# Reordering the opening of a conv-plus-FFN kernel, and the chunk work at its step ends

## The reference, cut to what matters

```
y   = grouped_conv1d(x, weight (128,32,9), groups=4, padding 4)   # x: (32 samples, 128 channels, 2048)
y   = y + (c @ c_weight.T)[:, :, None] + bias[None, :, None]
out = x + y @ kernel + ffn_bias                                   # kernel: (2048, 2048)
        + B_eff (A_eff y) + lora_B_shared (lora_A_shared y)
# A_eff, B_eff: one mix per group of 4 samples of 16 low-rank adapters (rank 32), weights `gate` (8,16)
```

## Time and profile before

| | |
|---|---|
| time, median of 3 runs | 1790.21 us (1789.97 to 1790.29) |
| profiled execution, its own time | 1793.14 us |
| its span, first to last instruction | 1791.3 us |
| mean granted clock of PE, share of full | 0.976 |
| PE busy | 1736.4 us, 97% |
| DVE, ACT, POOL busy | 1016.6, 669.3 and 189.5 us |
| moved by transfers | 411.22 MB |

### The profile page before, as it was taken

The page is one execution under the profiler, slowest core; times in us unless marked ns, Lnnn a source line. Parts: engine busy times, 40 slices in busy tenths (PEclk is TensorE's granted clock), DMA queues, the critical chain, the costliest instruction groups (busy, mean ns, idle before and its releaser), DMA issues.

```text
span 1791.3 us, 21987 instructions
## 1 busy us (share of the span) xinstructions
PE 1736.4 (97%) x8710; PEld 1487.9 (83%) x8710; DVE 1016.6 (57%) x1179; ACT 669.3 (37%) x841; POOL 189.5 (11%) x70
## 2 busy tenths in 40 slices
PE   6799899999999997999999999999999999999999
PEld 6688788878888887999999888888888888888887
DVE  3676765653544459999998423345555544453333
ACT  4556565653422256555564211122222311121110
POOL 0023422220000002222332100000000000000000
PEclk6699999999999998999999999999999999999999
DMA  8578768763666554887776654457776799886654
GB/s 213 152 245 286 254 224 276 260 207 118 203 222 218 198 186 172 327 299 277 259 250 247 224 191 148 178 179 243 240 229 217 246 338 315 307 287 206 195 197 149
DMA packets 182287, 411.22 MB, mean 230 GB/s; under 512 B 58724, under 2 KB 94404, under 8 KB 177544
## 3 DMA queue, kind: packets, MB, share of 16 engines
q1 hardware_dynamic: 182184, 409.81, 67.5%
HBM read 263.72 MB, written 146.03 MB: 229 GB/s over the span
## 4 chain that ended last, share of the span: by engine, by line
PE 87%; DVE 5%; DMA 4%; issue 2%; ACT 1%; SPq 1%; DVEq 0%; ACTq 0%
PE acc L1202 64%; PE cps L1104 14%; PE cps L1134 3%; PE acc L1120 3%; DVE x_q L838 2%; PE acc L1173 2%; DMA T<-g 2%; DMA mixed_B<-b_raw 2%; DVE g L862 1%; PE cps L1229 1%; DMA g<-in_L_ffn_lora_B_shared 1%; DVE x_lo L845 1%; ACT x_q L663 0%; ACT w_hi L655 0%; PE cps L1218 0%
## 5 line engine op out<-in xcount | busy, mean ns | idle before, releaser
L1202 PE MATMUL acc<-w_hi,y_t 128*128 128x512 f32 x3584 | 998.8, 393 | 10.0 <-DVE w_lo L828 6.9
L1202 PEld LDWEIGHTS acc<-w_hi,y_t 128*128 128x128 f32 x3584 | 669.4, 189 | 145.8 <-DVE w_lo L828 7.4
L1202 PE MATMUL acc<-w_lo,y_t 128*128 128x512 f32 x1792 | 556.2, 392 | 0.0
L1202 PEld LDWEIGHTS acc<-w_lo,y_t 128*128 128x128 f32 x1792 | 338.9, 189 | 71.8
L663 ACT COPY x_q<-x_raw 32x512 f32<-32x512 f32 x256 | 276.7, 1081 | 52.0 <-DVE x_lo L845 44.6
L1104 PE MATMUL cps<-cw_hi,x_hi 128*128 128x384 f32 (+2 forms) x768 | 232.2, 302 | 5.4 <-DVE x_lo L845 5.4
L1104 PE MATMUL cps<-cw_lo,x_hi 128*128 128x384 f32 (+2 forms) x768 | 232.0, 302 | 0.0
L1104 PE MATMUL cps<-cw_hi,x_lo 128*128 128x384 f32 (+2 forms) x768 | 231.3, 301 | 0.0
L692 ACT CAST y_t<-g 128x1024 fp32r<-128x1024 f32 x96 | 101.1, 1053 | 343.1 <-PE acc L1202 314.2
L927 DVE TENSOR_TENSOR g<-acc,g 128x1024 f32<-128x1024 f32 x96 | 117.0, 1220 | 171.5 <-PE acc L1120 113.0
L888 DVE TENSOR_TENSOR y_t<-g,y_t 128x1024 fp32r<-128x1024 f32 x96 | 119.4, 1244 | 133.2 <-ACT y_t L692 133.2
(11 more groups left out here) (94 smaller groups left out, 1057.2 us busy)
## 6 DMA issues: line engine op xcount, KB each, us to landing
g<-U SPq DMA_DIRECT2D x80, 512.0 KB, 5.7
x_raw<-in_x SPq DMA_DIRECT2D x32, 1024.0 KB, 6.4
g<-A SPq DMA_DIRECT2D x64, 512.0 KB, 5.2
g<-in_x SPq DMA_DIRECT2D x64, 512.0 KB, 6.3
out<-g SPq DMA_DIRECT2D x64, 512.0 KB, 3.4
A<-g SPq DMA_DIRECT2D x48, 512.0 KB, 5.1
S<-g SPq DMA_DIRECT2D x48, 512.0 KB, 3.0
U<-g SPq DMA_DIRECT2D x48, 512.0 KB, 4.1
```

The lines of the kernel that those rows point to most:

```text
L1202: ins = T.matmul(acc[:, b, m, :], y_buf[b][:, c, part, :], wt[:, k % SLOTS, m * 512:(m + 1) * 512], start=(c == 0 and part == 0 and wt is ...
```

## The change

The arithmetic stays the same apart from buffers and order.

- **Opening.** The first sample is loaded by ACT's queue. SP issues the small inputs, lora_A_shared, weight chunks 0 to 3 and then one slice of lora_A. The sample is rearranged and split group by group (`rearrange_0`, `split_0`), DVE taking 10 of the 16 copies and ACT 6, and `conv(0)` waits for one group at a time. PE then runs `conv(0)`, `mix_A(0)`, product 0, `mix_A(1)`, `conv(1)`, `mix_A(2)`, the transposes of the first lora_B slice, `mix_A(3)`, L1229, and the loop starts at step 1. `ax_part(0)` moves into product 1, after its third chunk. `mix_A(1)` writes banks of `cps` instead of `acc`.
- **lora_B_shared** is loaded, transposed, copied and stored in step 15 instead of in the opening.
- **Splits.** The `EARLY_SPLIT` chunks go to the end of a step on both engines. In step 31, the only step p = 15 that is followed by a convolution, chunks 3 and 4 join 5 to 7 at the end. The permuting copy of lora_B moves on ACT from before `x_split` to after `y_hi`.
- **Forming.** One call at each step's end, from step 1 to step 9: first the stores of chunk u-2, then the loads of chunk u-1.
- **Waits.** `ax_part(u)` waits for three of the four evacuated groups.

```diff
@@ SP, at each step's end
-            def forming(point):
-                j, part = (point - 1) // 3, (point - 1) % 3
-                if point >= 1 and j < NCH:
-                    if part == 0:
-                        load_forming(j)
-                    elif part == 2:
-                        store_formed(j)
+            def forming(u):
+                if 2 <= u <= NCH + 1:
+                    store_formed(u - 2)
+                if 1 <= u <= NCH:
+                    load_forming(u - 1)
@@ SP, opening
-            load_x(0)
...
-            load_lora_A(0)
-            load_lora_A(1)
             sp.dma_start(As_raw, lora_As).then_inc(as_raw_in, 16)
-            sp.dma_start(Bs_raw.rearrange("p (k r) -> p k r", r=RANK),
-                         lora_Bs.rearrange("(k p) r -> p k r", p=P)).then_inc(bs_raw_in, 16)
             for c in range(4):
                 load_t(0, c)
+            load_lora_A(0)
             sp.wait_ge(ctx_ready, 1)
             sp.dma_start(ctx_d, ctx_sum).then_inc(ctx_out, 16)
             sp.wait_ge(ctx_out, 16)
             load_ctx(0)
             load_ctx(1)
             load_x(1)
             for c in range(4, NCH):
                 load_t(0, c)
+            sp.wait_ge(as_done, 1)
+            load_lora_A(1)
+            load_lora_B(0)
+            store_y(0)
+            store_mixed_A(0)
+            load_lora_A(2)
+            load_x(2)
...
@@ ACT, opening
+            act.dma_start(x_raw[:], x[0]).then_inc(x_in, 16)
...
+            rearrange_0(0, (3,)).then_inc(q0_act, 1)
+            rearrange_0(1, (2,))
+            split_0(0)
+            rearrange_0(1, (3,)).then_inc(q0_act, 1)
+            split_0(1)
...
@@ DVE, opening
+            rearrange_0(0, (0, 1, 2))
+            rearrange_0(1, (0, 1))
+            split_0(0)
+            rearrange_0(2, (0, 1, 2))
+            split_0(1)
+            rearrange_0(3, (0, 1))
+            split_0(2)
+            split_0(3)
...
+            for i in range(GR):
+                split_t(0, i)
+                y_group(0, i)
+            y_lo(0)
+            for c in range(4, NCH):
+                split_t(0, c)
             a_mixed_copy(0)
             x_rearrange(1)
             x_split(1)
@@ PE, opening
-            mix_A(0)
-            mix_A(1)
-            conv(0)
-            mix_A(2)
-            mix_A(3)
-            pe.wait_ge(amix_act, RK)
-            pe.wait_ge(amix_dve, RK)
+            conv(0)
+            mix_A(0)
+            pe.wait_ge(gcol_ready, 1)
+            product(0)
+            mix_A(1)
+            conv(1)
+            mix_A(2)
+            turn_lora_B(0)
+            mix_A(3)
+            mix_B(0)
@@ DVE, a step
-                if f + 1 < 7 and p == NP - 1:
+                if f + 1 < 7 and p == NP - 1 and not has_conv(u + 1):
                     split_t(f + 1, 3)
                     split_t(f + 1, 4)
                 if has_conv(u + 2):
                     x_rearrange(conv_index(u + 2))
-                if f + 1 < 7 and p in EARLY_SPLIT:
-                    split_t(f + 1, EARLY_SPLIT[p])
...
+                if f + 1 < 7 and p in EARLY_SPLIT:
+                    split_t(f + 1, EARLY_SPLIT[p])
                 if f + 1 < 7 and p == NP - 1:
-                    for c in range(5, NCH):
+                    for c in range(3 if has_conv(u + 1) else 5, NCH):
                         split_t(f + 1, c)
@@ PE, ax_part
-                    pe.wait_ge(y_evac, min(4 * (u + 2), 4 * NP))
+                    pe.wait_ge(y_evac, min(4 * max(u + 1, 2) + 3, 4 * NP))
```

More of the change, by code:

```diff
@@ L568, in _ @@
                     load_sums(u + 1)
-                if u >= 1 and early(pu):
+                if early(pu):
                     store_stage(pu)
@@ L744, in _ @@
-            for c in range(4):
-                split_t(0, c)
-            a_mixed_copy(2)
-            a_mixed_copy(3)
-            y_hi(0)
+                    act.wait_ge(cwt_done, 3)
+                elif k >= 2:
+                    act.wait_ge(amix_out[k % 2], 32 * (k // 2))
+                src = cps[:, 3, :] if k == 1 else acc[:, 1, 0, :]
+                A.copy(a_stage[k % 2][:, 0].rearrange("p b (c r) -> p b c r", c=NCH),
+                       src.rearrange("p (c b r) -> p b c r", c=NCH, b=NB)).then_inc(amix_act, 1)
@@ new lines, in _ @@
+            act.wait_ge(x_in, 16)
+            act.wait_ge(edge_zero, 2)
+            rearrange_0(0, (3,)).then_inc(q0_act, 1)
[3 more added lines that the diff above has]
+            split_0(1)
+            rearrange_0(2, (3,)).then_inc(q0_act, 1)
+            split_0(2)
+            rearrange_0(3, (2, 3)).then_inc(q0_act, 1)
+            split_0(3)
+            for c in range(5):
+                split_t(0, c)
+            y_hi(0)
@@ L749, in _ @@
+            for c in range(5, NCH):
+                split_t(0, c)
+            a_mixed_copy(0)
             x_rearrange(1)
             x_split(1)
-            for c in range(4, NCH):
-                split_t(0, c)
-            for u in range(NU):
+            perm_lora_B(0)
+            a_mixed_copy(1)
+            x_rearrange(2)
+            x_split(2)
+            y_hi(1)
+            a_mixed_copy(2)
+            copy_turn(0)
+            a_mixed_copy(3)
+            for u in range(1, NU):
@@ L994, in _ @@
                 ins.then_inc(ones_ready, 1)
-            for c in range(4, NCH):
-                split_t(0, c)
-            for u in range(NU):
+            a_mixed_copy(1)
+            x_rearrange(2)
+            y_evacuate(1)
+            x_split(2)
+            y_lo(1)
+            a_mixed_copy(2)
+            a_mixed_copy(3)
+            copy_mixed_B(0)
+            for u in range(1, NU):
                 f, p = u // NP, u % NP
                 pu, pf = u - 1, (u - 1) // NP
-                if u >= 1 and pf in (2, 3):
+                if pf in (2, 3):
                     evac(pu)
-                if u >= 1 and pf in (1, 4):
+                if pf in (1, 4):
                     n = final_index(pu)
@@ L1220, in _ @@
-                if u == 0:
-                    conv(1)
-                    ax_part(0)
-                    pe.wait_ge(lb_perm, 1)
-                    for k4 in range(RK):
-                        ins = T.transpose(cps[:, 0, k4 * P:(k4 + 1) * P], lora_B_perm[:, k4, :], ident[:])
-                    ins.then_inc(bt_done, 1)
+                        turn_lora_B(u)
+                    if c == 5 and u == NP - 1:
+                        pe.wait_ge(bs_raw_in, 16)
+                        for k4 in range(4):
+                            ins = T.transpose(cps[:, 2, k4 * P:(k4 + 1) * P], Bs_raw[:, k4 * P:(k4 + 1) * P], ident[:])
+                        ins.then_inc(bs_done, 1)
@@ L1227, in _ @@
+            conv(0)
[8 more added lines that the diff above has]
+            mix_B(0)
+            for u in range(1, NU):
+                if has_conv(u + 1):
+                    conv(conv_index(u + 1))
+                product(u)
                 if u < NP:
-                    pe.wait_ge(bt_ready, u + 1)
-                    T.matmul(cps[0:NB * R8, 1, :], G[:].rearrange("p b r -> p (b r)"), b_turn, start=True, stop=True
-                             ).then_inc(bmix_done, 1)
+                    mix_B(u)
```

459 lines of the change are left out of this document (253 added, 206 removed).

## The result

| | before | changed |
|---|---|---|
| time, median | 1790.25 us (4 runs) | 1770.6 us (1769.02 to 1773.41, 4 runs) |
| ratio | 1 | 0.9888, 95% interval 0.9872 to 0.9904 |
| profiled execution, its own time / span | 1793.1 / 1791.3 us | 1771.0 / 1769.2 us |

The change makes the kernel 1.1% faster, 20 us, where 48 were forecast. All medians are of executions at a mean granted clock between 0.97 and 1.00; one of e7's four ran at 0.69, took 2286.7 us and is left out.

A forecast was written before the change was run, and what follows sets the result against it. PE, busy 97% of the span, was taken to bound the kernel. Gains of 32 (opening), 11.6 (phase 0) and 5 (step 31), less 0.5 (lora_B_shared), make 48: 1790.2 to 1742 us, range 1726 to 1762.

The forecast's parts named there:

- Step 1: Opening: `conv(0)` starts near 14 us and `conv(2)` at 72 instead of 103.96, a gain of 32 us.
- The bound of 84: Opening: latest start of `conv(2)`, 84 us, with all slices and two convolutions at the lower clock level.
- Step 2: Phase 0, `conv(2)` to `conv(15)`: moved splits take away stalls, 309.3 us against 320.9, a gain of 11.6.
- The slack: Phase 0: some 5 us between `mixed_B` landing and its due time, against 5.6 us of forming drift over eight steps.
- rival C: Phase 0: forming ring sets the pace, round 29.5 us, 1786 us; half-way, round 25.5, 12 lost, 1754; chance 0.20.
- Rival E: Phase 0: forming stores queue behind other transfers; slower from a round of 30 us, 1803 us at 32; chance 0.05.
- POOL beside DVE: Phase 0: if POOL's work slid onto DVE's copies, eight overlapped steps would add 8 to 24 us.
- Step 3: Step 31: DVE's idle for early splits goes, `conv(18)` comes 5 us earlier, bounds nothing and 13.
- Step 4: lora_B_shared in step 15: four transposes cost 0.5 us, the load lands beside product 15.
- B: Opening, phase 0 and step 31: less lost than charged, `conv(2)` at 65, no phase 0 stall, 1727 us; chance 0.15.
- D: Opening: clock stays at 1.2 GHz from 14 us on, `conv(2)` near 106, 1776 us; chance 0.10.
- The sum by the clock rule of the Trainium skill: Opening: sustained busy time lifts the clock, so slices run at full speed and `conv(2)` starts at 65 us.

The follow-up runs named there:

- e7: e3 with lora_A slices 2 and 3 copied by ACT and DVE into contiguous columns before PE uses them; 1754.3 us in three executions.
- e1: The changed kernel with four unused groups of 16 fp32 matmuls in phase 1, stationary columns at strides 16, 4, 2 and 1; 1798.0 us, one execution.
- e6: e3 with ACT's load of the first sample issued only when the conv weights have landed; 1753.8 us.
- e4: The kernel before with only the splits moved to the ends of steps and the permuting copy behind `y_hi`; 1772.8 us.
- e3: The changed kernel with the forming loads issued in the next step, behind the lora_B load and the `mixed_B` store; 1756.9 us.
- e2: The changed kernel with the forming schedule of before, a chunk each one and a half steps, loads first in step 0; 1767.5 us.
- e5: e3 with the four stores of shared_B issued by ACT behind its own copy; 1752.0 us.
- e8: e3 with the edits of e5, e6 and e7 together; 1748.5 us.

## Why the prediction was wrong

The direction was right, and one of the four terms. The size was not: the terms of the opening and of phase 0 were too high by 11 and 12 us, and that of `lora_B_shared` by 4.

**Step 1, the opening, 32 forecast, 20.6 measured.** The first term that failed is "four slices 14.0 (14.09 for two at half clock, if they scale)". They don't: 6.99 + 6.83 + 6.99 + 7.18 = 28.0 us. With the 3.5 us of clock that I had charged to the last, 17.5 stand against 28.0, so 10.5 of the 11.4 us missing. e1 shows why: the stationary operand is read at a stride of 16. The trace of before could have told the two readings apart: its third slice began at PEclk 1.00 and went no faster there, 0.19 us a record, and the pair 48.27 to 62.23 took 13.96 us with a mean PEclk of 0.62, against 14.09 at 0.50. My rows had the clock of the first pair only. The bound of 84, with all slices at the lower level, had their length right; that `conv(2)` came at 83.3, so near to it, is in part luck: the bound doesn't say what its two convolutions cost. `conv(0)` came 2.6 us later than 14, for the conv weights (e6 takes 2.4 of it back). Against this, the wait for `y_lo(0)`, 2.6, was none: the context landed in time, and PE came later. `conv(0)` took 12.05 for 12.2, product 0 12.28 for 13.5, `conv(1)` 11.64 for 10.9; the lora_B slice took 2.75 (0.85 and 1.90, at the lower clock) for 1.4. The differences sum to +10.5 + 2.6 - 2.6 - 0.15 - 1.2 + 0.7 + 1.35 = 11.2.

**Step 2, phase 0, 11.6 forecast, -0.7 measured.** The gain from the splits was right: e4 has 13.1. The step that failed is "The stores follow POOL one by one, so only the last one counts, 3 to 4 us: 24 us a round". The last store landed 6.2 to 8.8 us after POOL's end, 7.8 on average, and a round took 26.0; the other two terms were lower than I had them, 8.0 for 9.6 to POOL's start and 10.1 for POOL's 10.9. That the store is slow because it is queued behind the y stores and the next sample is argued, not tested. The slack was as small as I said, so the half-way case of rival C came true: it put a round at 25.5 and the loss at 12, and 15 more than e3 were lost at 26.0. I had named both pieces and gave them 0.20. How the round reached PE is SP's wait for that last store, with the loads behind it, ahead of the `mixed_B` store. That it is this order and not the volume is shown by e3, and that the loads alone don't do it by e2. Rival E's point, a round of 30 us, was not reached. POOL beside DVE cost little in the changed kernel; e2 shows it at its worst, 9.1 us in a single step, and there the trace agrees with the rule of the Trainium skill (SBUF — State Buffer, "SBUF: two separate sides") that DVE and POOL share a port pair and the one waits for the other's whole instruction: 5.70 us for two `x_lo` that took 2.39.

**Step 3, step 31, 5 forecast, 6.6 measured.** Right, with the mechanism: PE waits 6.48 us for `x_lo` before `conv(18)`. e4 gives 6.5 by itself.

**Step 4, lora_B_shared, -0.5 forecast, -4.2 measured.** The step that failed is the cost of 0.5: I costed the transposes and the load, and put the stores at nothing. SP stands at `bs_copied` until 439 us, and behind it are the last weight chunk, the `mixed_B` store and its round trip. On e3, where the stretch was 5.8 us above before's, e5 took back 3.6. The remaining 2.2 above before's 228.7 are the transposes (0.45), the wait of 1.4 us at the low-rank step, and 0.35 that I can't place.

**The rivals.** B did not happen. D, the clock low throughout, did not either: conv and product rows took 11.6 to 12.3 us, between the levels. But its symptom, slices at 7 us, was there for another reason. The sum by the clock rule of the Trainium skill (TensorE: Matmul & The Clock Gate, "Part 1: The HAM clock gate"), 65 for `conv(2)`, missed by more than mine, since it rested on slices that follow the clock.

What stays open: whether the 0.19 us a record of a strided group at full clock comes from the weight load or from the passes of the fp32 form was not taken apart; why the last formed store lands so late was not tested; and e7 alone was not told from e3.

## What to carry to other kernels

- Before a stretch at the lower clock is priced as "half of it at full clock", look for the same form of instruction at full clock, and cut the windows small enough to see the clock change inside it. The 7 us of a slice were a matter of the stride of its stationary operand.
- When a ring (load, work, store, load) shares a queue with small transfers that the critical engine waits for, issue the small ones before the queue's wait for the ring's last store. Moving that wait, with its four loads, behind two small transfers was worth 14 us here, with a DMA share of 0.95.
- A step that is moved out of an opening is not free where it lands: cost every transfer that it issues and what is queued behind the wait in front of them.

## What the runs showed of the hardware

- 16 fp32 matmuls of 64 columns (32 records) with a 128x128 stationary operand took 3.68 us with contiguous columns, 3.90 at a stride of 2 elements, 7.50 at 4 and 6.99 at 16, all beginning at PEclk 1.00; in the last two it fell to 0.50 within the group (e1). At 0.50 the contiguous form took 7.06 (e8).
- In a strided group PEclk stood at 1.00 from 511.7 to 514.7 us and at a mean of 0.58 from 514.7 to 518.7, and PE was busy for all of both stretches (e1).
- In the first 20 us of the changed kernel the windows print PEclk 1.00, but the first matmuls of `conv(0)` took 0.69 and 0.52 us; the same ones took 0.67 and 0.52 at 0.50 in the kernel before. Early in a trace, the length of a known matmul says more than the printed clock.
- With a DMA share of 0.95 to 0.98 for 23 us at a stretch, at up to 347 GB/s, PE did not have to wait (e3).
- The load of the conv weights took 5.17 us with the load of a sample issued beside it on another engine's queue (the changed kernel), and 2.18 with that load held back (e6).
